# The first mixture-of-experts stage: its full tiles listed from the counts of three batches, its matrix exponentials computed during the first attention

## The reference

```
x = x + attention0(ln(x))   16 heads, low-rank q and kv, rotary part, causal softmax over 1024 keys
x = x + experts0(ln(x))     router takes the best of 8 experts; silu(a) * g, 128 -> 2 x 512 -> 128
x = x + attention1(ln(x))   38 fixed offsets back (0 to 32, 48, 64, 96, 128, 192), gated
x = x + experts1(x)         2 of 8 experts, gelu; its output is multiplied by
                            expm(gens[0]) @ expm(gens[1]) @ expm(gens[2]), three 128 x 128 matrices
```

## Time and profile before

| what | value |
|---|---|
| runs | 1565.92, 1569.04 and 1569.08 us; median 1569.04 |
| the profiled execution's own time | 1560.68 us |
| its span, first to last instruction | 1558.9 us |
| granted TensorE clock, mean | 0.884 of full |
| PE busy | 1281.0 us, 82% of the span |
| DVE busy | 1159.4 us, 74% |
| ACT busy | 749.2 us, 48% |
| POOL busy | 690.9 us, 44% |

### The profile page before, as it was taken

How to read it: one execution, slowest core, us unless ns; L and a number is a source line. 1 busy time by engine, 2 the same in 40 slices (tenths; PEclk the granted TensorE clock), 3 DMA queues, 4 the chain that set the end, 5 groups by cost and what they waited for, 6 DMA issues and landing times.

```text
span 1558.9 us, 37842 instructions
## 1 busy us (share of the span) xinstructions
PE 1281.0 (82%) x13524; PEld 873.6 (56%) x13524; DVE 1159.4 (74%) x3814; ACT 749.2 (48%) x1523; POOL 690.9 (44%) x1004
## 2 busy tenths in 40 slices
PE   4499888988899888999896799939898989756890
PEld 2254544445445454554444698927777777655770
DVE  5588697896988969889774555538999998973556
ACT  1145555555555555555562255615544444215773
POOL 3023232233332333323321233348777888774664
PEclk9689999999999999999996699967888777568995
DMA  4765717556174571755705211102111112032335
GB/s 110 105 99 91 110 26 111 80 91 110 26 115 79 92 112 26 115 80 90 113 2 205 64 38 35 41 26 82 45 44 44 50 51 72 21 122 77 100 94 170
DMA packets 73881, 123.22 MB, mean 79 GB/s; under 512 B 17534, under 2 KB 46083, under 8 KB 72800
## 3 DMA queue, kind: packets, MB, share of 16 engines
q1 hardware_dynamic: 64472, 105.26, 35.6%
q0 software_dynamic: 7616, 13.59, 2.7%
q10 hardware_dynamic: 1608, 1.95, 0.7%
HBM read 30.40 MB, written 17.60 MB: 31 GB/s over the span
## 4 chain that ended last, share of the span: by engine, by line
PE 38%; DVE 32%; issue 10%; POOL 9%; DMA 4%; ACT 4%; DVEq 1%; SPq 1%; POOLq 0%; ACTq 0%
DVE first L795 5%; PE A L600 5%; PE S L1048 5%; PE S L583 4%; DVE S L798 4%; PE S L572 4%; POOL xq L1370 2%; PE A L1056 2%; DMA Qp<-mT 2%; DVE tA L774 2%; DVE tB L775 2%; PE S L564 2%; PE S L1560 2%; ACT P L685 2%; PE S L179 1%
## 5 line engine op out<-in xcount | busy, mean ns | idle before, releaser
L685 ACT ACTIVATE P<-S 128x512 f32<-128x512 f32 (+3 forms) x768 | 333.1, 491 | 279.8 <-PE S L583 275.2
L869 POOL TENSOR_SCALAR_AFFINE_SELECT P<-P 128x256 f32<-128x256 f32 (+1 forms) x256 | 116.8, 460 | 384.3 <-ACT P L685 384.0
L583 PE MATMUL S<-Qp,Kp 121*128 121x512 f32 (+3 forms) x768 | 251.6, 391 | 34.4 <-DVE tB L775 9.6
L572 PE MATMUL S<-Kp,Qp 120*128 120x512 f32 (+3 forms) x768 | 252.4, 398 | 33.4 <-DMA Kp<-rck 16.5
L798 DVE CUSTOM_DVE_ANT_0 S<-S,later 128x512 f32<-128x512 f32 (+3 forms) x512 | 239.0, 513 | 41.1 <-PE S L572 40.3
L572 PEld LDWEIGHTS S<-Kp,Qp 120*128 120x128 f32 x768 | 134.1, 196 | 166.8 <-issue 74.8
L583 PEld LDWEIGHTS S<-Qp,Kp 121*128 121x128 f32 x768 | 138.7, 192 | 111.1 <-issue 24.1
L795 DVE TENSOR_REDUCE first<-S 128x1 f32<-128x512 f32 x256 | 164.3, 683 | 47.4 <-PE S L572 47.1
L600 PE MATMUL A<-P,V 128*9 128x512 f32 (+3 forms) x1536 | 175.2, 505 | 6.0 <-POOL P L869 5.9
L2146 POOL DMA_INDIRECT yq<-yq,id x71 | 69.5, 979 | 44.5 <-DVE yq L2109 21.0
L1793 POOL TENSOR_TENSOR prod<-qf,kT 128x128 f32<-128x128 f32 x160 | 71.6, 481 | 36.0 <-ACT qf L1628 24.2
(11 more groups left out here) (333 smaller groups left out, 2700.4 us busy)
## 6 DMA issues: line engine op xcount, KB each, us to landing
Qp<-rcq SPq DMA_DIRECT2D x63, 256.0 KB
Kp<-rck SPq DMA_DIRECT2D x62, 256.0 KB
Qp<-rcq SPq DMA_DIRECT2D x63, 128.0 KB
Kp<-rck SPq DMA_DIRECT2D x62, 128.0 KB
xq<-xq SPq DMA_DIRECT2D x71, 72.0 KB
yb<-yq SPq DMA_DIRECT2D x8, 528.0 KB, 7.2
w<-in_w SPq DMA_DIRECT2D x4, 1024.0 KB, 10.0
Vo<-vt SPq DMA_DIRECT2D x32, 128.0 KB
```

Source lines behind the costliest of these rows:

```text
L572: te.matmul(S[s][:, 512 * h:512 * h + n], Q[0:120, h, 128 * qt:128 * qt + 128], K[0:120, h, 512 * part:512 * part + n], start=True, stop=T ...
L583: te.matmul(S[s][:, 512 * h + c:512 * h + 512], K[0:121, h, 128 * kb:128 * kb + 128], Q[0:121, h, 512 * qh + c:512 * qh + 512], start=True ...
L685: se.activation(k.P[(w.n - 1) % NP0][:, h, c:512], S[s][:, 512 * h + c:512 * h + 512], ACT.Exp, scale=SCALE0).then_inc(p.done("st").h, 1)
L869: ge.affine_select(P[:, :, start:c + 128], P[:, :, start:c + 128], [[0, 2], [1, wide]], ALU.is_ge, 0.0, base=start - c, channel_multiplier ...
```

## The change

`FULL0` is 17. The first three batches have 3072 tokens over 8 experts. Whatever the counts, at least 17 whole tiles of 128 rows can be filled from them. Their expert and row are worked out by the first call of the new function `tiles0` (part 0), placed in the last unit of the first attention. The other 22 tiles are worked out by the second call (part 1), when the last batch's counts are known.

- The three exponentials move into the first attention. G0, gT and "ex" 8 to 1 go into the first batch's chain and its first maxima, fT with the first squaring and the other nine squarings, R1 and R go to the 12 steps in `POWERS`, in units 0, 2, 3 and 4. The adding of the identity's multiples, which was in DVE instructions, is now an extra matmul against the identity ("ex" 6 matmuls in place of 3, "sq" 9 in place of 6, the last one 12), and the read-outs are ACT copies. `gm` is loaded at the start, the third DMA of SP's queue.
- SP loads the experts' constants and 6.3 MB of weights in the first attention, as soon as the last unit's q and k have landed, then writes one pad block, waits for the scatters of three batches and for the first `tiles0`, and loads six tiles' rows ahead of the barrier.
- In the experts' stage the tiles start at once. The last batch's routing stands beside tiles 0 to 7, the second `tiles0` behind tile 7. SP's queue is: tiles 6 to 11, the next stage's constants, tiles 12 to 16, the eight pad blocks, tiles 17 to 38. POOL's scatters of results and of the last batch's rows are now in the list's order.
- The four memsets of `Kp` on POOL go behind the first layer norm's POOL work. The SBUF tiles of the stages are laid into three shared rooms (`big`, `low`, `mid`), so that the weights fit beside what is still in use. Tiles of the second attention and second experts lie in them too, their instructions unchanged.

The diff, cut to its core:

```diff
+FULL0 = -(-((B - 1) * T - 8 * 127) // 128)
...
+        self.big = self.sb(ctx, "big", [128, 12288])
+        self.low = self.sb(ctx, "low", [128, 2048])
+        self.mid = self.sb(ctx, "mid", [128, 2048])
...
-        ge.indirect_dma_start(r.xs, bass.IndirectOffsetOnAxis(r.posu[q][:, i:i + 1], 0), r.xr[q][:, i, :], None).then_inc(p.sem("d_sc0").h, 16)
+        ge.indirect_dma_start(r.xs, bass.IndirectOffsetOnAxis(r.posu[q][:, i:i + 1], 0), r.xr[q][:, i, :], None).then_inc(p.sem("d_sc3" if q else "d_sc0").h, 16)
...
+SQ, DEG = 10, 9
+POWERS = [(0, 1), (0, 4), (0, 7)] + [(2, n) for n in (1, 4, 7, 10)] + [(3, n) for n in (1, 4, 7, 10)] + [(4, 1)]
...
+            if (u, step) in POWERS:
+                next(steps, None)
...
+        def exponentials():
+            o.add("G0")
+            o.add("gT", ring="S")
+            for d in range(DEG - 1, 0, -1):
+                o.add("ex", d, ring="S")
+                yield
+            o.add("fT", ring="S")
+            for n in range(SQ):
+                o.add("sq", n, ring="S")
+                yield
+            o.add("R1", ring="S")
+            yield
+            o.add("R", ring="S")
+
+        steps = exponentials()
+        next(steps)
+        first("fuse", "ln1", "ln2", "ln3", "ln4")
+        next(steps)
+        first("xnT")
+        next(steps)
+        first(("rope", "cq", 0), ("spin", "cq", 0), ("high", "cq", 0))
+        next(steps)
+        first(("rope", "cq", 1), ("spin", "cq", 1), ("high", "cq", 1), "kv")
+        next(steps)
+        first(("low", "cq", 0), "cq", "kv2", ("low", "cq", 1))
+        next(steps)
+        first(("rope", "ck", 0))
+        next(steps)
+        first(("spin", "ck", 0), ("high", "ck", 0), "kv3", "kvT", ("rope", "ck", 1), ("spin", "ck", 1), ("high", "ck", 1), ("low", "ck", 0), "ck",
               ("low", "ck", 1), "v")
         for i in range(12 + EARLY):
             maxima(i // 12, i % 12)
+            if i == 5:
+                next(steps)
         for u in range(NU):
             for step, _ in enumerate(attend(u)):
                 i = 12 * (u + 1) + step + EARLY
                 if i // 12 <= NU:
                     maxima(i // 12, i % 12)
                 beside(u, step)
+                if (u, step) == (NU - 1, 10):
+                    o.add("tiles0", 0)
...
         ye.dma_start(p.x[:, 4 * i:4 * i + 4, :], x_in[:, 4 * i:4 * i + 4, :]).then_inc(p.sem("d_x").h, 16)
...
+    for u in range(NU - 4, NU):
+        shipped(p, sp, u, "cq", "ck")
+    for n in f0.loads:
+        ye.dma_start(f0.small[n], a[n][:, 0:f0.small[n].shape[1]]).then_inc(p.sem("d_f0").h, 16)
+    for e in range(4):
+        ye.dma_start(f0.w1[:, 2048 * e:2048 * e + 2048], a["w1"][:, 2 * e:2 * e + 2, :].rearrange("p e n -> p (e n)")).then_inc(p.sem("d_w0").h, 16)
+        ye.dma_start(f0.w2[:, 1024 * e:1024 * e + 1024], a["w2"][:, 2 * e:2 * e + 2, :, :].rearrange("p e j n -> p (e j n)")).then_inc(p.sem("d_w0").h, 16)
+    xs = k.route.xs
+    sp.wait_ge(p.sem("d_f0"), 16 * len(f0.loads))
+    ye.dma_start(xs[8 * CAP:8 * CAP + 128, :], f0.small["pads"]).then_inc(p.sem("d_pad0").h, 16)
+    sp.wait_ge(p.sem("d_sc0"), SENT0)
+    sp.wait_ge(p.sem("v_row0"), 1)
+    for t in range(NX):
+        row = ye.value_load(f0.rowi[0:1, t:t + 1], min_val=0, max_val=8 * CAP)
+        ye.dma_start(f0.xg[t], xs[bass.ds(row, 128), :]).then_inc(p.sem(f"d_xg{t}").h, 16)
 
 
 CONSTS0, WEIGHTS0 = 16 * 4, 16 * 5
...
+        elif w.kind == "ex":
+            pe.wait_ge(p.done("gT"), 1)
+            if w.n > 1:
+                pe.wait_ge(p.done("ex"), w.n - 1)
+            for i in range(3):
+                te.matmul(S[s][:, 128 * i:128 * i + 128], k.GT[:, i, :], k.F[:, i, :], start=True, stop=False)
+                ins = te.matmul(S[s][:, 128 * i:128 * i + 128], p.ident[:], k.G[:, i, :], start=False, stop=True)
+            ins.then_inc(p.made("ex").h, 1)
+        elif w.kind == "fT":
+            pe.wait_ge(p.done("ex"), DEG - 1)
...
+        elif w.kind == "sq":
+            n = w.at[0]
+            f, e = k.F, k.E
+            pe.wait_ge(p.done("fT"), 1)
+            if n:
+                pe.wait_ge(p.done("sq"), n)
+            for i in range(3):
+                te.matmul(S[s][:, 128 * i:128 * i + 128], f[:, i, :], e[:, i, :], start=True, stop=False)
+                te.matmul(S[s][:, 128 * i:128 * i + 128], p.ident[:], k.twice if n < SQ - 1 else p.ident[:], start=False, stop=True)
+            for i in range(3):
+                ins = te.matmul(S[s][:, 512 + 128 * i:640 + 128 * i], e[:, i, :], f[:, i, :], start=True, stop=n < SQ - 1)
+                if n == SQ - 1:
+                    ins = te.matmul(S[s][:, 512 + 128 * i:640 + 128 * i], p.ident[:], p.ident[:], start=False, stop=True)
+            ins.then_inc(p.made("sq").h, 1)
+        elif w.kind == "R1":
+            pe.wait_ge(p.done("sq"), SQ)
+            te.matmul(S[s][:, 0:128], k.F[:, 1, :], k.E[:, 0, :], start=True, stop=True).then_inc(p.made("R1").h, 1)
+        elif w.kind == "R":
+            pe.wait_ge(p.done("R1"), 1)
+            te.matmul(S[s][:, 0:128], k.F[:, 0, :], k.F[:, 2, :], start=True, stop=True).then_inc(p.made("R").h, 1)
...
+        elif w.kind == "G0":
+            act.wait_ge(p.sem("d_gm"), 16)
+            act.wait_ge(p.sem("d_id"), 16)
+            se.activation(k.G, k.E, ACT.Copy, scale=float(2.0 ** -SQ)).then_inc(p.sem("a_G").h, 1)
+            se.activation(k.F, k.E, ACT.Copy, scale=float(2.0 ** -SQ / DEG))
+            se.activation(k.twice, p.ident[:], ACT.Copy, scale=2.0)
...
+        elif w.kind == "ex":
+            act.wait_ge(p.made("ex"), w.n)
+            se.activation(k.F, S[s][:, 0:384].rearrange("p (g d) -> p g d", g=3), ACT.Copy, scale=1.0 / w.at[0]).then_inc(p.done("ex").h, 1)
...
+        elif w.kind == "sq":
+            act.wait_ge(p.made("sq"), w.n)
+            se.activation(k.E, S[s][:, 0:384].rearrange("p (g d) -> p g d", g=3), ACT.Copy)
+            se.activation(k.F, S[s][:, 512:896].rearrange("p (g d) -> p g d", g=3), ACT.Copy).then_inc(p.done("sq").h, 1)
...
+        elif w.kind == "tiles0":
+            dve.wait_ge(p.sem("d_f0"), 16 * len(f0.loads))
+            dve.wait_ge(p.made("rope"), 16 * B)
+            dve.wait_ge(p.made("v"), B)
+            dve.wait_ge(p.done("rk"), 2 * (B - 1))
+            tiles0(p, dve, ve, f0, 0)
...
-    ge.memset(k.kvT[:], 0.0).then_inc(p.sem("g_kvT0").h, 1)
-    for V in k.V:
-        pool.then(ge.memset(V[:, :, :, 8:9], 1.0))
-    for i in range(4):
-        pool.then(ge.memset(k.K[i][96:128, :, :].bitcast(F32), 1.0))
-    ge.memset(p.half[:], -0.5).then_inc(p.sem("g_ones").h, 1)
-    ge.memset(k.P[1][:, :, 0:256], 0.0).then_inc(p.sem("g_P1").h, 1)
...
+    pool.then(ge.memset(k.V[0][:, :, :, 8:9], 1.0))
...
+            if w.n == 1:
+                pool.wait_ge(p.sem("g_rstd"), 1)
+                for i in range(4):
+                    pool.then(ge.memset(k.K[i][96:128, :, :].bitcast(F32), 1.0))
+                ge.memset(p.half[:], -0.5).then_inc(p.sem("g_ones").h, 1)
+                ge.memset(k.P[1][:, :, 0:256], 0.0).then_inc(p.sem("g_P1").h, 1)
...
+        elif w.kind == "R":
+            pool.wait_ge(p.done("R"), 1)
+            ge.memset(k.V[1][:, :, :, 8:9], 1.0).then_inc(p.sem("g_ones").h, 1)
...
@@ -961,41 +1090,45 @@
                 o.add("up", t - 1, ring="S")
             if t >= DD:
                 o.add("down", t - DD, ring="A")
-            if t % 2:
-                next(steps, None)
-        all_of(steps)
+            for half in beside.get(t, ()):
+                next(half)
+            if t == 7:
+                o.add("tiles0", 1)
+        all_of(one, two)
         return o.items[start:]
+
...
     for n in one.wt:
         ye.dma_start(one.wt[n][:], a[n]).then_inc(p.sem("d_a1").h, 16)
     for t, n in ((one.bias, "bias1"), (one.ms, "ms"), (one.near, "near"), (one.far, "far"), (one.blk, "blk")):
         ye.dma_start(t[:], a[n]).then_inc(p.sem("d_a1").h, 16)
-
-    sp.wait_ge(p.sem("d_f0"), 16 * len(k.small))
-    xs = k.route.xs
-    ye.dma_start(xs[8 * CAP:8 * CAP + 128, :], k.small["pads"][:]).then_inc(p.sem("d_pad0").h, 16)
+    for t in range(NX + 6, FULL0):
+        load(t)
     sp.wait_ge(p.sem("v_end0"), 1)
     for e in range(8):
         end = ye.value_load(k.endi[0:1, e:e + 1], min_val=0, max_val=8 * CAP - 128)
-        ye.dma_start(xs[bass.ds(end, 128), :], k.small["pads"][:]).then_inc(p.sem("d_pad0").h, 16)
+        ye.dma_start(xs[bass.ds(end, 128), :], k.small["pads"]).then_inc(p.sem("d_pad0").h, 16)
     sp.wait_ge(p.sem("d_pad0"), 16 * 9)
-    sp.wait_ge(p.sem("d_sc0"), 16 * NT)
-    sp.wait_ge(p.sem("v_row0"), 1)
-    for t in range(NE):
-        if t >= NX:
-            sp.wait_ge(p.made("turn"), t - NX + 1)
-            sp.wait_ge(p.sem("g_id"), t - NX + 1)
-        row = ye.value_load(k.rowi[0:1, t:t + 1], min_val=0, max_val=8 * CAP)
-        ye.dma_start(k.xg[t % NX][:], xs[bass.ds(row, 128), :]).then_inc(p.sem(f"d_xg{t % NX}").h, 16)
```

(31 more changed lines are left out.)

262 lines of the change are left out of this document (124 added, 138 removed).

## The result

| | before | after |
|---|---|---|
| median of runs | 1569.06 us (4 runs, 1565.92 to 1569.39) | 1541.77 us (4 runs, 1539.11 to 1546.71) |
| profiled execution | 1560.68 us | 1539.84 us |
| its span | 1558.9 us | 1538.1 us |
| granted clock, mean | 0.884 | 0.893 |
| PE, DVE, ACT, POOL busy | 1281.0, 1159.4, 749.2, 690.9 us | 1280.1, 1152.3, 763.4, 695.4 us |

The ratio is 0.9834 (95% interval 0.9804 to 0.9865): 27 us faster by the medians, where 24 were predicted. A later set of runs gave 1544.2 against 1565.05 us, ratio 0.9862 (0.9831 to 0.9893), 21 us. The predicted difference lies between the two; the predicted time, 1545, lies 3 us and 1 us above the two medians.

A forecast was written before the change was run, and what follows sets the result against it. PE was taken to bound the tiles and nearly the attention units, with an idle gap between. Terms -47.3 - 2.9 + 23.2 + 1 + 1.5 + 0.5 = -24 took the median 1569.04 to 1545 us; range 1534 to 1557.

The forecast's parts named there:

- The gap, -47.3: Between the last addition to x and the first tile matmul: the idle time goes, 47.3 us saved.
- The tiles' stretch, -2.9: First experts' tile loop, 134.0 us: exponentials' work leaves, routing, clock and DVE costs come in, net 2.9 us less.
- The term for DVE's second list: First nine tiles: DVE is full and the second `tiles0` is 5 us in one piece; 3 us taken, 0 to 8.
- The clock's term: Start of the tiles: PE runs at the low clock until it returns; 4 us taken, between 1.5 and 6.
- The routing's term: Tiles' stretch: PE's router matmuls, transpositions and ranks for the routing come in, 4 us.
- The exponentials, +23.2: First attention's units: 101 added matmuls of 22.5 us, plus copy waits, less 2 hidden in PE's idle, 23.2 us.
- The rival by latency, 4.3: Units: each squaring costs its latency, 4.3 us, not its work; time 1575 us; chance 6%.
- the absorption of 40%: Rival in the units: PE's idle hides 40% of the added matmuls; time 1532 to 1536 us; chance 14%.
- The first chain, +1: First batch's chain, up to and beside the first maxima: added "ex" steps cost 1 us, ends -4 and +7.
- The weights' load, +1.5: Last unit of the first attention: the 6.3 MB load meets one mT DMA, 1.5 us taken, +3 at once needed.
- The tail, +0.5: End of the first attention: `tiles0` on DVE, hidden by its wait for PE except last small instructions, 0.5 us.
- Units 5 to 30, unchanged: Sign in the first attention's profile: these units keep their length, all growth lying before unit 5.

The follow-up runs named there:

- routing_first: Changed kernel, but the tile loop begins only behind both halves' last routing and the whole tile list: 1570.95 us, ratio 1.0038 to the kernel before.
- lists_in_three: Changed kernel with the second tile list on VectorE cut into three pieces, behind tiles 7, 8 and 9: 1536.34 us, ratio 0.9809 to the kernel before.
- only_gT_and_R: Changed kernel without Taylor steps, fT, ten squarings and R1, R's product behind the first chain's queries' products: 1518.91 us, ratio 0.9726 to the kernel before.

## Why the prediction was right

- **The gap, -47.3.** Measured -47.4 in both pairs of traces. The predicted first tile matmul, 2.9 us behind the addition, came 2.84 behind it. The loads were thought to be just in time: the first `tiles0` was to end 9.7 us ahead of the last addition's end and the loads' issue 2.7 ahead. Measured: 10.1 (848.6) and 3.9:

```profile
848.88 5.94 SPq L575 DMA_DIRECT2D mid<-xs  x6
```

- **The tiles' stretch, -2.9.** Measured -3.3 and -2.7. The term for DVE's second list, "I take 3", is the wait of 3.15 us and its slow tile, and the kernel that cuts the list got 3.6 back. The clock's term was taken at 4; by the rows the stretch has half a microsecond at 0.50 and 5 us at 0.76, a loss of about 1.5. The routing's term was 4 as well. The stretch without routing and list took 121.8 (routing_first), with the routing and the list in pieces 127.2 (lists_in_three), so the routing cost about 5.4. That the total came out is in part luck: one term was 2.5 too high, two together 2 too low.
- **The exponentials, +23.2.** Units 0 to 4 grew from 119.2 to 140.5 us (means of two and of five traces), 21.3. Without them (only_gT_and_R) the units took 21.9 less. Per squaring 2.3 and 1.6 against the 2.0 of the sum. The rival by latency, 4.3, did not come, nor the absorption of 40%.
- **The first chain, +1.** mT of unit 0 moved from 75.5 to 77.4, +1.9: 0.4 of it up to the first maxima (62.0 to 62.4), 1.5 from there (13.5 to 15.0 us; means of two and of five traces). Two steps in the term were wrong. One put "ex" 1, which lies beside the first maxima, at 0. ScalarE copies its product only behind four of its own DMA issues, and PE waits for that copy, 0.84 to 2.40 us in the five traces:

```profile
63.60 7.63 ACTq L812 DMA_DIRECT2D Kp<-big  x4
71.28 0.49 ACT L760 ACTIVATE V<-S 128x384 f32<-128x384 f32 x1 [22.31 <-issue]
...
71.82 1.82 PE L680 MATMUL S<-Kp,Qp 120*128 120x512 f32 x7 [1.84 <-ACT V L760]
```

The other is "the layer norm is also 3 us sooner, with POOL's memsets behind it". POOL's reciprocal root is 3 us sooner. VectorE's normalisation behind it runs beside the memsets. Before:

```profile
6.33 3.66 POOL L840 MEMSET Kp<- 32x2048 f32 x2
...
12.78 2.14 DVE L158 TENSOR_SCALAR tA<-x,mv,rs 128x128 f32<-128x128 f32 x8 [5.40 <-POOL rs L153]
```

and after:

```profile
9.73 7.47 POOL L984 MEMSET Kp<- 32x2048 f32 x4
9.79 7.56 DVE L173 TENSOR_SCALAR tA<-x,mv,rs 128x128 f32<-128x128 f32 x8 [2.25 <-POOL rs L168]
```

The same eight instructions take 7.56 us in place of 2.14, as long as the four memsets, which keep their 1.87 us each. They end at 17.35 where they had ended at 14.92: 3 us sooner became 2.4 later. PE's transposition behind them starts at 18.06 in place of 15.06. By the first maxima all but the 0.4 had been made up. The Trainium skill (SBUF — State Buffer, Who interferes with whom) says that `tensor_scalar` can use the port pair that VectorE shares with GpSimd, and that whoever comes second is then blocked for the whole instruction. The rows agree: the memsets start first, and only VectorE is slowed. The same operation on `xr`, from 861.8 to 867.8 with no memset beside it, takes 0.34 us each; here one takes up to 1.90. A kernel with the memsets elsewhere was not tried, so what it would bring is open.
- **The weights' load, +1.5.** Measured +3.6 (22.9 us from mT 30 to mT 31, the mean of the four traces in the table with the changed kernel's units and load, against 19.3), and all of it given back when the load moved. The term was less than half of what it cost, and the bound of +3 was passed: the product behind the transfer came 5.8 us after its issue, where 4.6 had served as the longest. That a DMA engine takes turns between queues packet by packet (the Trainium skill, DMA: Bandwidth & Descriptors, Queues, rings and completion order) was read as speaking for a small price. The trace agrees in that mT did not wait for the whole load: its product started at 815.22, and the load's last DMA, issued at 804.28, landed 15.6 us later. mT came 3 us later than without the load all the same.
- **The tail, +0.5.** Measured +0.4 from mT 31 to the last addition (27.3, the mean of the same four, against 26.8).
- **Units 5 to 30, unchanged.** 593.2 us (five traces) against 591.1 (two): 2.1 more with the same instructions, about the scatter between two traces of one kernel (592.1 and 590.0 before, 592.1 and 593.7 after). Not explained further.
- **The second half, unchanged.** The pair of first profiles had 5.9 us more after the change, the second pair 0.6.

Of the signs named beforehand, one did not come as written: from the first maxima to the last addition the time grew by 28.8 us (means of two traces each), not 23 to 25, and 6.2 of it lie behind mT of unit 5.

The two pairs of profiled executions differ by 20.8 and 15.6 us, the medians by 27 and 21. The stages' means up to the end of the first experts give 1.9 + 21.3 + 2.1 + 3.6 + 0.4 - 47.4 - 3.0 = -21.1. The sum of -24 was 3 us too good: the exponentials were taken 2 us too dear, the load, the chain and the unchanged units 5 us too cheap. That the time came closer is luck. The prediction added the 8.4 us by which the median of the kernel before lies above its profiled execution. After the change the median lies only 1.9 us above.

## What to carry to other kernels

Work moved from an idle stage into a busy one costs its time on the bound engine there, less what is idle. Here that was 21 us in the units, against 25 us or more that it had cost in its old place. The rest of the gain, 26 us or less, came from letting the tiles start ahead of the routing. Look for the true hole first: here it was where the first transfers are awaited, and fT and four squarings cost 2 us there. Put a long piece of work on an engine that feeds the bound one as several short pieces between its results. Before you put a small read-out on an engine, see whether it issues DMAs there.

## What was not expected of the hardware

- VectorE's eight normalisations took 3.5 times as long (7.56 in place of 2.14 us) with memsets of GpSimd beside them, and GpSimd's memsets kept their 1.8 to 1.9 us.
- A 6.3 MB load through SyncE's queue lengthened the time from the issue of a transfer in GpSimd's queue to the product behind it from 2.6 to 5.8 us.
- Four DMA issues held ScalarE for 7.6 us, and a copy of 0.49 us behind them held PE up for 1.84 us.
- The granted clock at one place differs between executions of one program, and the time of the same instructions with it: unit 0 of the changed kernel took 29.0 us at 0.96 in one trace and 30.0 at 0.88 in the other. From mT 5 to the last addition the eight traces in the table with the weights' load where the change put it have 640 to 646 us.
